# A two-layer transformer kernel: the shared expert's normed rows come back from memory instead of from VectorE

## The reference, cut to what matters

```python
# x: (16, 112, 256), ctx: (16, 375, 256)
x = x + L0_xcond(layernorm(x), cond, ctx)      # self attention, cross attention, gated MLP
x = x + L0_ffn(layernorm(x))                   # 64 experts, 8 of them for each row, + a shared one
x = x + L1_xcond(ctx, layernorm(x), cond, cond)
x = x + L1_ffn(layernorm(x))                   # 8 experts, one for each row

def L0_ffn(h):                                 # h = layernorm(x), 16 x 112 rows of 256
    affinity = sigmoid(h @ router_w)
    top_scores, top_idx = top_k(affinity, 8)
    shared = (silu(h @ shared_gate_w) * (h @ shared_up_w)) @ shared_down_w
    routed = sum over the 8 chosen experts of weight * expert(h)
    return shared + routed
```

## Time and profile before

| | us |
|---|---|
| median of three timed executions | 3120.73 |
| profiled execution | 3111.76 |
| its span | 3110.0 |
| TensorE busy in it | 2822.0 |
| VectorE busy | 1508.2 |
| ScalarE busy | 1047.6 |
| GpSimd busy | 902.5 |

### The profile page before, as it was taken

How to read it: one execution, slowest core, us unless ns; L and a number is a source line. 1 busy time by engine, 2 the same in 40 slices (tenths; PEclk the granted TensorE clock), 3 DMA queues, 4 the chain that set the end, 5 groups by cost and what they waited for, 6 DMA issues and landing times.

```text
span 3110.0 us, 58302 instructions
## 1 busy us (share of the span) xinstructions
PE 2822.0 (91%) x17275; PEld 1937.6 (62%) x17276; DVE 1508.2 (48%) x4412; ACT 1047.6 (34%) x2721; POOL 902.5 (29%) x1782
## 2 busy tenths in 40 slices
PE   7999999999999999995999948999999999999696
PEld 5776667666766766664788725555555555555464
DVE  4454555554455455555555424554445544554232
ACT  1343333333333333331333303433334333343121
POOL 0021221211221122213555444344433444320111
PEclk9999999999999999997999978999999999999798
DMA  6000000000000000003788821000000000000431
GB/s 212 8 6 6 6 6 6 6 6 6 6 2 6 5 6 6 6 2 115 218 258 259 138 98 36 19 19 25 28 20 18 18 27 26 20 2 2 134 140 59
DMA packets 89264, 154.75 MB, mean 50 GB/s; under 512 B 16964, under 2 KB 64720, under 8 KB 87664
## 3 DMA queue, kind: packets, MB, share of 16 engines
q1 hardware_dynamic: 39760, 85.60, 8.6%
q0 software_dynamic: 21072, 42.53, 5.9%
q10 hardware_dynamic: 28368, 25.83, 2.5%
HBM read 121.93 MB, written 31.98 MB: 49 GB/s over the span
## 4 chain that ended last, share of the span: by engine, by line
PE 38%; DVE 5%; issue 5%; DMA 2%; POOL 1%; ACT 1%; DVEq 1%; ACTq 0%; POOLq 0%
PE psG L886 7%; PE psG L892 7%; PE psG L1217 5%; PE psG L1294 2%; PE psO L1309 2%; PE psO L1229 2%; DVE nmax L1789 2%; PE psG L902 2%; PE psG L838 2%; PE psT L853 2%; PE psO L866 2%; PE psG L880 2%; PE psG L1208 1%; DMA kT<-normed_rows,ids 1%; DVE X L2234 1%
## 5 line engine op out<-in xcount | busy, mean ns | idle before, releaser
L1437 ACT ACTIVATE probs<-psG,nmax 112x375 f32<-112x375 f32 (+1 forms) x512 | 317.2, 620 | 268.3 <-DVE nmax L1789 268.3
L892 PE MATMUL psG<-W,ctxT 128*125 128x512 f32 (+2 forms) x896 | 403.9, 596 | 0.0
L886 PE MATMUL psG<-ctxT,W 128*128 128x375 f32 (+1 forms) x1024 | 391.4, 530 | 1.1 <-ACT ctxT L1624 1.1
L853 PEld LDWEIGHTS psT<-ident,probs 112*125 112x125 f32 (+2 forms) x1792 | 205.0, 167 | 215.6 <-ACT probs L1437 134.5
L1789 DVE TENSOR_REDUCE nmax<-psG 112x1 f32<-112x375 f32 (+1 forms) x512 | 285.6, 599 | 90.2 <-PE psG L838 90.1
L880 PE MATMUL psG<-hT,W 128*128 128x112 f32 x2560 | 309.9, 280 | 18.7 <-ACT hT L1462 17.7
L880 PEld LDWEIGHTS psG<-hT,W 128*128 128x128 f32 x2560 | 297.1, 195 | 35.6 <-ACT hT L1462 26.9
L853 PE MATMUL psT<-ident,probs 112*125 112x112 f32 (+2 forms) x1792 | 261.6, 280 | 50.8 <-ACT probsT L1445 32.1
L886 PEld LDWEIGHTS psG<-ctxT,W 128*128 128x128 f32 x1024 | 189.6, 190 | 165.7 <-issue 114.3
L892 PEld LDWEIGHTS psG<-W,ctxT 128*125 128x125 f32 (+2 forms) x896 | 160.5, 186 | 180.7 <-issue 178.9
L838 PE MATMUL psG<-kT,qT 64*112 64x375 f32 (+1 forms) x1024 | 250.5, 567 | 11.3 <-ACT ctxT L1624 10.7
(11 more groups left out here) (346 smaller groups left out, 4094.0 us busy)
## 6 DMA issues: line engine op xcount, KB each, us to landing
expert_rows<-kT ACTq DMA_DIRECT2D x197, 128.0 KB, 1.8
W<-in_ew SPq DMA_DIRECT2D x64, 384.0 KB, 4.6
W<-in_ew SPq DMA_DIRECT2D x8, 2048.0 KB, 8.8
ctxT<-in_ctxT SPq DMA_DIRECT2D x16, 375.0 KB, 3.1
kT<-in_ctx SPq DMA_DIRECT2D x16, 375.0 KB
W<-in_eb SPq DMA_DIRECT2D x8, 640.0 KB, 10.0
normed_rows<-hrow SPq DMA_DIRECT2D x32, 112.0 KB, 1.9
kT<-normed_rows,ids POOLq DMA_INDIRECT x197, 4.1
```

What stands on the lines that cost most here:

```text
L853: mm = nc.tensor.transpose(psT[0:kn, i, c * T:(c + 1) * T], probs[:, 2 * (u % 2) + i, k0:k0 + kn], ident[0:T, 0:T])
L886: mm = nc.tensor.matmul(bank[:, 0:n], wt[:, c, n0 + j * P:n0 + (j + 1) * P], src[:, c, 0:n], start=(c == 0), stop=(c == DC - 1))
L892: mm = nc.tensor.matmul(bank[0:kn, 0:512], src[:, c, k0:k0 + kn], wt[:, c, n0 + half * 512:n0 + (half + 1) * 512], start=(c == 0), stop=(c ...
L1437: nc.scalar.activation(probs[:, 2 * (s % 2) + i, 0:keys], psG[0:T, score_banks(s)[i], 0:keys], ACT.Exp, bias=nmax[:, h:h + 1], accum_out=r ...
```

## The change

SyncE reads `hall` back from `normed_rows` in two transfers: batches 0 to 14 after the shared weights, as soon as the first 15 stores have landed, and batch 15 behind its own store, once that has landed. The 16 VectorE instructions go, and so do the two GpSimd copies into `mur` and `rsr` of each tile, which nothing reads any more. TensorE waits once for both transfers, where it waited for each batch.

```diff
@@ SyncE
             sp.dma_start(shw, a["shw"]).then_inc(sh_in, 16)
+            sp.wait_ge(S0.h_stored, 16 * B)
+            sp.dma_start(hall[:, 0:B - 1, :], hd.rearrange("(b t) d -> t b d", t=T)[:, 0:B - 1, :]).then_inc(S0.sh_rows, 16)
             store_rows(B - 1)
+            sp.wait_ge(S0.h_stored, 16 * B + 16)
+            sp.dma_start(hall[:, B - 1, :], hd.rearrange("(b t) d -> t b d", t=T)[:, B - 1, :]).then_inc(S0.sh_rows, 16)
@@ GpSimd, normalise_tile
-                nc.gpsimd.tensor_copy(mur[:, bass.ds(r, 1)], mv[0:T, 1, 0:1])
-                nc.gpsimd.tensor_copy(rsr[:, bass.ds(r, 1)], ry[0:T, 1:2])
@@ TensorE, shared
-                        pe.wait_ge(s.sh_rows, b + 1)
+                        if b == 0:
+                            pe.wait_ge(s.sh_rows, 32)
@@ VectorE, shared
-                dve.wait_ge(s.normed, B)
-                for b in range(B):
-                    nc.vector.tensor_scalar(hall[:, b, :], X[:, b, :], mur[:, b:b + 1], rsr[:, b:b + 1], ALU.subtract,
-                                            ALU.mult).then_inc(s.sh_rows, 1)
```

## The result

The changed kernel takes 3125.14 us (median of 20 runs, 3122.27 to 3129.14) where the kernel before takes 3119.82 us (20 runs, 3113.91 to 3123.15) beside it: a ratio of 1.0019, 95% interval 1.0012 to 1.0026. It is some 5 us slower, where 3.3 us less had been forecast. Its profiled execution took 3123.19 us.

What follows compares the result with a forecast made beforehand. Bound: VectorE's sixteen instructions and GpSimd's transfers, meeting at the block tables' cast. VectorE's -4.8 us (0.27 included), less a 1.5 us wait for the gather, gave -3.3: 3120.73 to 3117.4 us; range 3114.9 to 3122.6.

Steps and rivals of the forecast that it cites:

- step 5: VectorE's cast of the gathered block tables at 1462.96, within 19 steps to the routed experts; two paths arrive within 0.1 us.
- GpSimd's two copies, -0.27: On tile 15, dropping GpSimd's two copies brings the block tables 0.27 us earlier; on tiles 0 to 14 it changes nothing.
- VectorE, -4.8: Without the sixteen instructions VectorE's first shared-expert copy starts near 1447.0 instead of 1451.80: -4.8 us, including the 0.27.
- Without the stop: eighth scatter at 1448.85: GpSimd's 4.96 us stop before tile 15's eighth scatter goes, so that scatter starts at 1448.85 instead of 1454.08.
- the second explanation: VectorE's sixteen instructions, in a two-port mode, keep GpSimd from writing descriptors; the 4.96 us stop would go with them.
- Its landing under full DMA engines took 4.4 us: The eighth scatter lands in 4.4 us again, at 1453.25; the gathered tables land by 1459.7, and VectorE waits 1.5 us.
- Four loads 1.6 to 5.5 us late. Cost: nothing directly: Layer 1's three weights and the context go out 1.6 to 5.5 us late behind SyncE's reads; no direct cost.
- the third: Rival: delayed loads run into the expert weights, stop kept, tables 2.0 us late, TensorE's clock falls: 3124.2 us; chance 0.09.
- Its clock term: In the slower rival, TensorE idles some 5 us before the cast, then runs 3 us at half speed: 1.5 us.
- The reads' own cost: Both reads of hall land by 1431.3 to 1435.5, TensorE needs them at 1446.4: hidden by 11 us or more.

Runs made afterwards that it cites:

- the quiet order: Changed kernel, expert weight loads held until the block tables' gather has landed, layer 1's three weight loads moved behind the first of them: 0.9988 of the kernel before, twice.
- The own semaphore: Changed kernel with the last tile's eight scatters counted on a separate semaphore: 3233.18 us once on another chip; timed later, 1.0002 of the kernel before.
- The run with the weights held back: Changed kernel, SyncE issuing the first eight expert weight loads only once the block tables' gather has landed: 1.0005 of the kernel before.
- the run with the last read behind the loads: Changed kernel with the last batch's read of hall put behind layer 1's three weight loads and the context: 1.0004 of the kernel before.

## Why the prediction was wrong

**What bounds, and the two paths into step 5: right.** The sixteen lay on the path, and the block tables' path through GpSimd was the other one. That both arrive in step 5 together held for one execution only: in the second profile of that kernel VectorE waits 2.13 us there for the block tables, so GpSimd's path was the later one before the change made it longer.

**GpSimd's two copies, -0.27: right in size.** From M, `gcol` starts at 25.26 and 25.32 in the two profiles before and at 25.04 after: 0.22 to 0.28 us earlier.

**VectorE, -4.8: right.** The first copy stands at M + 30.7 before and at M + 26.05 after, -4.7. In the quiet order some 4 of these us arrive at the routed experts and in the time.

**"Without the stop: eighth scatter at 1448.85": this step failed.** It put at nothing a stop that stayed. The eighth scatter was to start at M + 27.8 and started at M + 38.2 (1457.27). I had seen the stop of 4.96 us and put it down to a fetch of instructions or to VectorE's sixteen, both of which the change takes away or shifts. The 8 KB packet just ahead of the restart was a coincidence: in the kernel before profiled again it comes behind the restart, in the quiet run too, and moving the code did not move the stop. The changed kernel, which has no sixteen and a stop twice as long, speaks against the sixteen. The own semaphore, with the same work on VectorE and no stop, rules out that VectorE's work alone holds GpSimd. So the rule of the Trainium skill (SBUF — State Buffer, "SBUF: two separate sides") that VectorE in a two-port mode keeps GpSimd from writing descriptors, which I had weighed as the second explanation, does not account for this stop. The eighth waits for the seventh's landing, and only while the last tile is counted on `scat_a`. The change did not touch that count, and the length of the stop follows how late the seventh lands.

**"Its landing under full DMA engines took 4.4 us": the second failure, in size.** Full is not one state. Eight us from the seventh scatter on, of the kernel before, of the changed one, of the changed one with its own semaphore, and of the quiet one (stretch, us, busy us of the engines, TensorE's granted clock, DMA share, GB/s):

```profile
1447.57:1455.57 8.00, 3.46 (x13) 2.61 (x12) 5.58 (x18) 0.28 (x1) 1.98 (x2) 0.53 0.84 254
```

```profile
1445.57:1453.57 8.00, 7.56 (x31) 5.61 (x31) 3.85 (x15) 1.73 (x7) 0.92 (x1) 0.78 0.90 84
```

```profile
1449.75:1457.75 8.00, 7.58 (x31) 5.63 (x31) 3.87 (x17) 1.72 (x7) 1.87 (x2) 0.77 0.88 92
```

```profile
1449.20:1457.20 8.00, 7.63 (x31) 5.60 (x31) 3.86 (x15) 1.54 (x7) 2.57 (x3) 0.77 0.01 1
```

The share is nearly the same, 0.84 and 0.90, but the bytes are a third: 84 GB/s against 254. The context's rows of 1 KB are now moved in this stretch, with the expert weights beside them. The expert weights' packets of 3 KB took 356 ns on average between M + 18 and M + 37, where they took 155 before. Under that the seventh scatter lands 9.7 us after its start (at M + 36.2), where it took 4.3. Without the stop each takes longer to land than the one before it: 4.7 us for the first, 8.3 for the eighth. Hence, with the own semaphore, the gather comes at M + 37.2 and not at the M + 33.0 of my sum (1454.0), and there is no gain.

**"Four loads 1.6 to 5.5 us late. Cost: nothing directly": the size was right, 3.9 us, the cost wrong.** I had asked only who waits for these loads, and no one does. What they share costs: the DMA engines, in the us in which GpSimd's scatters must land. The run with the weights held back and the quiet one (on another chip) differ in layer 1's three loads alone. With these out of the way too, the seventh lands in 2.1 us instead of 6.4, the cast comes 3.7 us earlier, and the ratio is 0.9988 where it was 1.0005. How much of the loss is due to the 3.9 us of delay is not shown, since the run with the last read behind the loads decides nothing.

**The rivals.** What happened is closest to the third, to which I gave 0.09: loads moved back run into the expert weights, the stop is kept, the tables are late, TensorE idles and its clock falls. It gave 3.5 us more than before, where 5.3 were measured. That its 3124.2 lies within 1 us of 3125.14 is partly luck: the three runs it started from have a median 0.9 us above that of the twenty. It kept the stop at its old length and had the block tables only 2.0 us late. From M the cast is 6.2 us later than in the profile that I forecast from (48.1 against 41.9) and 3.6 later than in the second one (44.5). Its clock term was 1.5: from cast to routed experts it is 23.13 us after and 21.67 before, +1.46. The stretch behind the cast, before and after, in eight us, and four us of the latter:

```profile
1462.00:1470.00 8.00, 7.58 (x42) 5.66 (x40) 6.74 (x36) 2.44 (x9) 6.00 (x16) 1.00 0.02 5
```

```profile
1466.00:1474.00 8.00, 5.99 (x20) 4.46 (x21) 4.65 (x25) 0.80 (x3) 5.88 (x17) 0.56 0.02 5
1467.00:1471.00 4.00, 2.99 (x9) 2.14 (x10) 3.12 (x18) 0.00 (x0) 2.32 (x12) 0.50 0.00 0
```

Behind the 9.26 us of idle time the granted clock of TensorE is 0.50 (1.2 GHz) for these four us and 0.56 over the eight, where it was 1.00 (2.4 GHz) before. From M the routed experts start 7.7 us later than in the first profile before and 5.0 later than in the second; the medians differ by 5.3. The range did not hold the time because I cut the third rival off half way: its condition, a stop that stays, was one that I had explained away without a test.

**The reads' own cost: right.** Both have landed long before the tables; TensorE's first transposes start at 1444.38, behind `gcol`.

**What stays open.** It is open why the scatter that brings `scat_a` to 2048 waits until the seventh has landed, and 1.99 us more, while the gather that brings `yk_in` to 2048 does not: the count, the kind of transfer and GpSimd's own wait behind it are not told apart. A run with the scatters as they are, and the wait for 2048 on another engine or behind the gathers, would tell. It is also open why the seventh takes 6.4 us to land with the expert weights held back, when the last packets of 1 KB, the context's, are over at M + 28.3, 4.5 us ahead of the landing.

## What to carry to other kernels

When work moves from an engine to transfers, price the transfers by what shares the DMA engines with them, not only by who waits for them: here small, late scatters on the critical path were stretched by loads that no engine was waiting for at that time. A stop without a semaphore in the trace is a term of the sum that must be tested before a forecast takes it away; over several executions its length against the last landing tells more than what stands next to it in one. A gain on one of two paths that meet needs the other shortened as well: the reads pay (0.9988, three times) once the large loads leave the scatters alone, where the same order of loads without the reads gives 1.0002.

## What the runs showed of the hardware

- The scatter of GpSimd that takes `scat_a` from 2032 to 2048 starts 1.99 us after the landing of the one before it, in twelve of twelve executions, with no wait ahead of it in the program. With the last eight counted on another semaphore it follows by 1.25 us. A gather that takes another semaphore to 2048 follows by 1.24 us with the one before it still under way, so the count alone is not the cause.
- DMA engines 0.90 busy moved 84 GB/s in one stretch and 254 GB/s at 0.84 in another. Scatters of 112 words landed in 2.1 us on idle engines, in 4.3 in the second of these stretches and in 9.7 in the first.
- An idle time of TensorE turns into a second loss behind it. With the cast waiting 3.3 us or more, the granted clock of the eight us behind the cast is 0.54 to 0.79, and the way from the cast to the routed experts takes 22.6 to 24.3 us; the four longest (23.7 and more) are those with a clock of 0.54 to 0.57. With no wait, or one of 2.13 us, the clock is 1.00 and the way takes 21.3 to 22.1 us.
